# Last unit's additions of attention shared by two engines, and the next stage's weights and first block fetched during them

## What is computed

```python
xn = layernorm(x)
s = lightning_attention(xn)          # layer 0: 16 heads of 32, decayed, chunked
g = silu(bitlinear_ffn(xn))          # 512 -> 2048 -> 512, ternary weights
x = x + s * g
xn = layernorm(x)
q, k, v = xn @ wq.T, xn @ wk.T, xn @ wv.T     # layer 1: 16 heads of 32, rope on q, k
att = softmax(rope(q) @ rope(k).T / sqrt(32))
s = (att @ v) @ wo.T
gate = silu(xn @ ((wq_gate - 128) * s_gate).T)     # 512 -> 1408
up = xn @ ((wq_up - 128) * s_up).T
g = silu((gate * up) @ ((wq_down - 128) * s_down).T)
out = x + s * g
```

## Time and profile before

| what | us |
|---|---|
| runs | 3112.64, 3121.56, 3123.32 (median 3121.56) |
| the profiled execution | 3116.13 |
| its span, first to last instruction | 3114.0 |
| TensorE busy | 2878.6 (92%) |
| VectorE busy | 1842.0 (59%) |
| GpSimd busy | 1425.2 (46%) |
| ScalarE busy | 1298.4 (42%) |

### The profile page before, as it was taken

How to read it: one execution, slowest core, us unless ns; L and a number is a source line. 1 busy time by engine, 2 the same in 40 slices (tenths; PEclk the granted TensorE clock), 3 DMA queues, 4 the chain that set the end, 5 groups by cost and what they waited for, 6 DMA issues and landing times. The chain is left out here.

```text
span 3114.0 us, 54321 instructions
## 1 busy us (share of the span) xinstructions
PE 2878.6 (92%) x19392; PEld 2017.0 (65%) x19392; DVE 1842.0 (59%) x2701; ACT 1298.4 (42%) x2015; POOL 1425.2 (46%) x1006
## 2 busy tenths in 40 slices
PE   6999999699999994799999999999999669999999
PEld 5878878588888873455555555555554248788887
DVE  5657676577777653566666666666666144444444
ACT  3211111366666651255555555555555522222222
POOL 2014555122333320177777777777777812222222
PEclk9999999899999997699999999999999979999999
DMA  3211121122222323122222222222221052322221
GB/s 122 89 54 61 54 67 41 34 85 81 96 86 85 101 78 133 41 69 69 69 69 69 69 68 75 83 72 70 77 72 32 25 192 88 95 95 81 88 88 47
DMA packets 151494, 238.98 MB, mean 77 GB/s; under 512 B 13232, under 2 KB 78896, under 8 KB 151344
## 3 DMA queue, kind: packets, MB, share of 16 engines
q1 hardware_dynamic: 149904, 235.45, 22.9%
q10 hardware_dynamic: 1440, 1.33, 0.1%
HBM read 178.02 MB, written 58.72 MB: 76 GB/s over the span
## 5 line engine op out<-in xcount | busy, mean ns | idle before, releaser
L1170 DVE TENSOR_REDUCE l_attn_maxima<-l_attn_ps_max 128x2 f32<-128x1024 f32 x512 | 626.9, 1224 | 247.9 <-PE l_attn_ps_max L1222 235.6
L1143 POOL TENSOR_TENSOR l_attn_summed<-l_attn_summed,l_attn_probs 128x1024 f32<-128x1024 f32 x256 | 601.4, 2384 | 56.6 <-ACT l_attn_probs L1094 56.6
L1094 ACT ACTIVATE l_attn_probs<-l_attn_ps_sc 128x1024 f32<-128x1024 f32 x512 | 497.6, 1028 | 124.4 <-PE l_attn_ps_sc L1210 123.8
L1143 POOL TENSOR_TENSOR l_attn_summed<-l_attn_probs 128x1024 f32<-128x1024 f32 x128 | 302.8, 2391 | 334.0 <-ACT l_attn_probs L1094 334.0
L62 PE MATMUL l_attn_ps_prep<-l_attn_wqkv_hi,l_attn_xt 128*128 (+1 forms) x1024 | 286.1, 362 | 37.8 <-DMA l_attn_xt<-xt_chunks 21.3
L1423 POOL TENSOR_TENSOR l_ffn_ht_lo<-l_ffn_mixed,l_ffn_ht_hi 128x512 fp32r<-128x512 f32 x88 | 114.0, 1295 | 451.5 <-ACT l_ffn_ht_hi L1444 451.5
L1222 PEld LDWEIGHTS l_attn_ps_max<-l_attn_qk_hi 32*128 32x128 f32 x1024 | 97.2, 185 | 305.3 <-DVE l_attn_maxima L1170 294.1
L1222 PE MATMUL l_attn_ps_max<-l_attn_qk_hi 32*128 32x512 f32 x1024 | 240.0, 463 | 48.5 <-DVE l_attn_maxima L1170 25.4
L1232 PE MATMUL l_attn_ps_y<-l_attn_probs,l_attn_v 128*32 128x512 f32 x2048 | 273.4, 606 | 1.1 <-ACT l_attn_probs L1094 1.1
L1101 ACT ACTIVATE l_attn_x_tok<-l_attn_ps_prep 128x256 f32<-128x256 f32 x128 | 49.2, 385 | 445.9 <-DVE l_attn_ps_prep L1159 445.9
L62 PEld LDWEIGHTS l_attn_ps_prep<-l_attn_wqkv_hi,l_attn_xt 128*128 128x128 f32 x1024 | 185.7, 196 | 74.4 <-issue 32.1
(11 more groups left out here) (231 smaller groups left out, 6212.1 us busy)
## 6 DMA issues: line engine op xcount, KB each, us to landing
l_attn_xt<-xt_chunks SPq DMA_DIRECT2D x128, 512.0 KB, 3.6
xt_chunks<-l_ffn_xt SPq DMA_DIRECT2D x32, 512.0 KB, 4.6
l_ffn_xt<-xt_chunks SPq DMA_DIRECT2D x32, 512.0 KB, 5.9
l_attn_xin<-in_x SPq DMA_DIRECT2D x32, 256.0 KB, 4.3
...
s<-l_attn_s_sb SPq DMA_DIRECT2D x32, 256.0 KB, 2.2
...
l_ffn_xa<-in_x SPq DMA_DIRECT2D x32, 256.0 KB, 2.7
```

Of the source, the lines that this page charges most:

```text
L1094: act.activation(probs[kt % RING][:, hs, :], ps_sc[:, hs, :], ACT.Exp, scale=ATT_SCALE).then_inc(exp_done, 1)
L1143: pool.tensor_tensor(total[:, hs, :], old[:, hs, :], probs[kt % RING][:, hs, :], ALU.add).then_inc(added, 1)
L1170: dve.tensor_reduce(maxima[b][:, j, PAIR * hp:PAIR * hp + PAIR, half:half + 1], ps_max[:, :, :], AX.X, ALU.max).then_inc(max_read, 1)
```

## The change

Four things change, all in layer 1.

1. In the last unit (m = 15) the additions of a quad are shared: GpSimd adds the first pair of heads (L1143's line, now with one turn of the loop), VectorE the second (`late_add`), one step later in its program; a semaphore `added_late` counts them, and ScalarE (the exponential four steps on), and TensorE (the sum over the partitions) wait for both.
2. In ticks 16 and 17 SyncE's queue fetches gate and up in eight pieces of 128x1408 and Wo in two of 128x1024 into two buffers `ffn_raw`, and the first four chunks of x; VectorE makes the weights of them in its steps 12 to 21 (`ffn_piece`). They lie in tiles that both stages use: `w_tile` (before it holds the attention's projection weights), `x_tiles` (the attention's four `xt`), `wo_hi` and `wo_lo` (one of its two pairs of `qk`).
3. The preparation block of the feed-forward is gone. Down is fetched in four pieces in its first block and made by VectorE after j = 6, 8, 9 and 10; the scales are fetched at the stage's start by ScalarE's queue, and ScalarE and VectorE wait for all three before their first work.
4. A chunk of x is now contiguous in its tile, and the moving operand of gate and up, `x_tiles[:, :, half, k, :]`, consists of four pieces of 128 columns.

```diff
-def layer1_attention(nc, xt_in, wqkvT, rope_cos, rope_sin, yt_out, den_out):
+def layer1_attention(nc, xt_in, wqkvT, rope_cos, rope_sin, yt_out, den_out, woT, gateT, upT, x_tiles, w_tile, wo_hi, wo_lo):
...
+        FFN_PIECES = 2 * KD + 2
...
+            n = STEPS * (t - NT) + s - 12
+            return n if 0 <= n < FFN_PIECES else None
...
+            def load_raw(n):
+                need(sp, ffn_made, n - 1)
...
             def tick(t, p):
+                late = isinstance(t, int) and t >= NT
                 load(t, 0)
                 store(t - 2, 0, y_copied, y_sb, yt_out)
...
+                if late and t == NT:
+                    load_raw(0)
+                    load_raw(1)
+                    load_ahead()
+                if late and t == NT + 1:
+                    load_raw(6)
+                    load_raw(7)
                 store(t - 2, 0, den_read, den_sb, den_out)
+                if late and t == NT + 1:
+                    load_raw(8)
+                    load_raw(9)
...
                 store(t - 2, 1, den_read, den_sb, den_out)
+                if late and t == NT:
+                    for n in range(2, 6):
+                        load_raw(n)
...
-                        for i in range(HPG // PAIR):
+                        for i in range(1 if shared(m) else HPG // PAIR):
...
+            def late_add(qb, kt):
+
+                m, hs = NT - 1, slice(PAIR, HPG)
+                total = summed[qb][kt // PER_SUM]
+                need(dve, exp_done, 2 * quad_index(m, qb, kt) + 2)
...
+                dve.tensor_tensor(total[:, hs, :], old[:, hs, :], probs[kt % RING][:, hs, :], ALU.add).then_inc(added_late, 1)
+
+            def ffn_piece(n):
+
+                dve.wait_ge(raw_ld[n % 2], 16 * (n // 2 + 1))
+                if n == 0:
+                    dve.wait_ge(proj_done, CPB * NT)
+                if n < 2 * KD:
+                    dve.tensor_scalar(ffn_matrix(n), ffn_raw[n % 2][:, :], ZERO_POINT, None, ALU.subtract).then_inc(ffn_made, 1)
...
+                        if m == NT - 1 and kt % PER_SUM:
+                            late_add(qb, kt)
+                        n = ffn_piece_at(t, s)
+                        if n is not None:
+                            ffn_piece(n)
...
-                sp.dma_start(raw_o[:, :, :], w_rows(woT)).then_inc(wo_in, 16)
-                sp.dma_start(raw_gate[:, :, :], w_rows(gateT)).then_inc(gate_in, 16)
-                sp.dma_start(raw_up[:, :, :], w_rows(upT)).then_inc(up_in, 16)
-                sp.dma_start(raw_down[:, :, :], w_rows(downT)).then_inc(down_in, 16)
-                load_xt(sp, 0)
...
+        PIECE = 3
+        PIECE_AFTER = {6: 0, 8: 1, 9: 2, 10: 3}
...
+            act.dma_start(sc_down[:, :], s_down.rearrange("(a n) -> a n", a=1).to_broadcast([P, DIM])).then_inc(scales_in, 16)
+            act.wait_ge(scales_in, 48)
...
-                        mm = pe.matmul(out_bank[:, :], w[:, k, P * j:P * j + P], xt[:, half, k, :], start=(k == half == 0), stop=(k == KD - 1 and half == 1))
+                        mm = pe.matmul(out_bank[:, :].rearrange("p (c n) -> p c n", n=P), w[:, k, P * j:P * j + P], x_tiles[:, :, half, k, :], start=(k == half == 0), stop=(k == KD - 1 and half == 1))
...
-                        need(pe, xt_ld, 16 * CB * (t + 1))
+                        need(pe, xt_ld, 16 * CB * t)
...
+                    if isinstance(t, int) and t == i == 0:
+                        pe.wait_ge(down_made, len(PIECE_AFTER))
```

More of the change, by code:

```diff
@@ L973, in layer1_attention @@
         den_done, den_read, y_copied = sem("den_done"), sem("den_read"), sem("y_copied")
+        added_late, raw_ld, ffn_made, wo_hi_made, x_ahead = sem("added_late"), [sem(f"raw_ld{i}") for i in range(2)], sem("ffn_made"), sem("wo_hi_made"), sem("x_ahead")
         block = ctx.enter_context(nc.Block())
@@ L1034, in adds_with, with shared, shared_adds, ffn_matrix @@
             return ADDS * (QB * m + qb) + PAIR * ((PER_SUM - 1) * (kt // PER_SUM) + r)
+        def shared(m):
+            return isinstance(m, int) and m == NT - 1
+        def shared_adds(qb, kt):
+            return ADDS // PAIR * qb + (PER_SUM - 1) * (kt // PER_SUM) + max(kt % PER_SUM, 1)
+        FFN_PIECES = 2 * KD + 2
+        def ffn_matrix(n):
+            return w_tile[:, HID * n:HID * (n + 1)] if n < 2 * KD else None
+        def ffn_piece_at(t, s):
+            if not isinstance(t, int) or t < NT:
+                return None
+            n = STEPS * (t - NT) + s - 12
+            return n if 0 <= n < FFN_PIECES else None
         def parity(p, back):
@@ L1086, in tick @@
                         if not isinstance(m, int) or n >= RING:
-                            if qb == 0 and kt < RING:
+                            if shared(m) and (qb or kt >= RING):
+                                qb_was, kt_was = (CPB * qb + kt - RING) // CPB, (kt - RING) % CPB
+                                need(act, added, ADDS * QB * m + shared_adds(qb_was, kt_was))
+                                need(act, added_late, shared_adds(qb_was, kt_was))
+                            elif qb == 0 and kt < RING:
                                 need(act, added, adds_with(m - 1, 1, kt + RING))
@@ L1257, in prepare @@
                 else:
-                    need(pe, added, ADDS * (QB * m + i + 1))
+                    if shared(m):
+                        need(pe, added, ADDS * QB * m + ADDS // PAIR * (i + 1))
+                        need(pe, added_late, ADDS // PAIR * (i + 1))
+                    else:
+                        need(pe, added, ADDS * (QB * m + i + 1))
                     for k in range(SUMS):
@@ new lines, in load_xt, with piece_of @@
+                sp.dma_start(fp32(x_tiles[:, i, :, :, :]).rearrange("p h k n -> p (h k n)"),
+                             xt_in[src if isinstance(t, int) else sp.snap(src)]).then_inc(xt_ld, 16)
+        PIECE = 3
+        PIECE_AFTER = {6: 0, 8: 1, 9: 2, 10: 3}
+        raw_down = two("raw_down", [P, PIECE, DIM], I32)
+        raw_ld = [sem(f"raw_ld{i}") for i in range(2)]
+        down_made, scales_in = sem("down_made"), sem("scales_in")
+        def piece_of(n):
+            return slice(PIECE * n, min(PIECE * n + PIECE, KH))
@@ L1394, in store, with load_down, prologue @@
                 sp.dma_start(out_t[c if isinstance(t, int) else sp.snap(c)], res[b][:, :]).then_inc(stored[b], 16)
+            def load_down(n):
+                need(sp, down_made, n - 1)
+                ks = piece_of(n)
+                sp.dma_start(raw_down[n % 2][:, 0:ks.stop - ks.start, :], w_rows(downT)[:, ks, :]).then_inc(raw_ld[n % 2], 16)
+            def prologue():
+                for i in range(2):
+                    sp.dma_start(yt[i][:, :, :], yt_in[i]).then_inc(yt_den_ld[i], 16)
+                    sp.dma_start(den[i][:, :, :], den_in[i]).then_inc(yt_den_ld[i], 16)
+                load_down(0)
+                load_down(1)
             def tick(t, p):
```

96 lines of the change are left out of this document (52 added, 44 removed).

## The result

In the same rounds the kernel before took 3118.3 us and the changed one **3074.2 us** (medians of four runs each; 3068.8 to 3078.5), a ratio of 0.986 [0.983, 0.988]. The forecast was 3084, range 3072 to 3093.

A forecast was written before the change was run, and what follows sets the result against it. TensorE was busy 92% of the span but idle while the feed-forward's weights were transferred and waiting on GpSimd in attention's tail. 33.3 + 0.8 = 34.1 us off 3118.4 gave 3084.3, taken as 3084; range 3072 to 3093.

The forecast's parts named there:

- term 1: Start of layer 1's feed-forward: the preparation block leaves TensorE's path, 33.8 less 0.5 for a barrier, gaining 33.3 us.
- two bounds: Limits for the preparation block's gain: 33.83 us if the barrier costs nothing, 32.2 if TensorE starts 1.7 us late.
- The cover: Attention's tail and feed-forward's start: the moved fetches, conversions and scales are hidden behind other work, cost taken as 0.
- rival of a rough entry: Feed-forward's start: scales land late (2.4 us), TensorE's first product 1.7 instead of 0.5 us after the barrier; 3088, chance 0.15.
- term 2: Tail of layer 1's attention: VectorE and GpSimd share additions but exclude each other, gaining 0.8 us; range 0 to 7.1.
- nineteen instructions of the sum: Attention's tail: six GpSimd and six VectorE additions, three conversions, two casts, two subtractions, one after another, 27.7 us.
- rival of free engines: Attention's tail: VectorE and GpSimd do not exclude each other, sharing gains 7.1 us, 3078 in all; chance 0.22.
- The seams: Gate and up's four-piece operand: no cost expected; rival over 8 ns a seam is slower, chance 0.04, between without change 0.02.
- The body: Feed-forward from its first gate product to the end: no change forecast (0), matmuls 0.2325 us apart, 73 us a block.

## Why the prediction was right or wrong

- **The preparation block** (term 1): right. 33.3 us forecast, 33.8 measured (the stretch took 35.4 to 38.2 us in the other runs that keep the block). The 0.5 us that I charged for the barrier was not there: TensorE's first product starts 0.05 us behind the queue's first issue. Of the two bounds the outer one, 33.83, was met.
- **The cover.** The ten pieces cost nothing by themselves; VectorE waited up to 0.54 us for one, and the products with v kept their step of 3.33 us, but for one of 3.85, which the rows before have too (20.48 us for six). The scales landed 7.2 us after their issue, 8.04 us behind TensorE's start, and the silu that waited for them was late by 0.1 to 0.2 us, not by 2.4. The rival of a rough entry falls. (Its 2.4 is a slip: 11.3 less 9.05 is 2.25, which moves the high end of the range by 0.15.)
- **The shared additions** (term 2): the mechanism was right, the size was off: 0.8 us forecast, 1.9 measured. The nineteen instructions of the sum do follow each other, but from 2449.22 to 2475.82, in 26.6 us instead of 27.7. The sum took each at its full length; nine of them stood behind the other engine, and each of these needed 0.12 to 0.13 us less than that once released (VectorE's addition 1.08 us instead of 1.21, GpSimd's 2.24 instead of 2.36). The rival of free engines falls: with nothing else in the tail sharing gives 6.0 us, and the work on the weights takes 4.0 of them. The Trainium skill (SBUF — State Buffer, Who interferes with whom) says that either engine stands behind the other, whichever came first. No row before showed GpSimd standing; now one does (3.43 us at 2456.40 behind VectorE's 1.21, against 2.35), and the measurement agrees with it. GpSimd stands behind conversions too, as the run in which it adds everything shows: the second of its two additions at 2473.37 begins at 2476.69, 0.60 us before VectorE's cast is through (2477.29), and takes 2.84 us instead of 2.35.
- **The seams**: right: four runs of 128 columns take the time of one run of 512 (3121.7 us beside 3122.0). The runs don't test the reason given, beyond that.
- **The body** was the miss: "the product's matmuls 0.2325 us apart as now". The step that failed is in the treatment of part 4 of the change: the prediction asked what the shape of the moving operand would cost, and put the tile's new place at nothing without a reason. Eight matmuls take 1.82 us instead of 1.86, 1408 x 5 ns = 7.0 us. Moving x in the kernel before shows it. With this term the sum would have been 3118.4 - 34.1 - 7.1 = 3077.2, against 3074.2 measured.

The range held the time only because its low end was taken from another rival, the free engines, which did not happen: the forecast itself from the lowest run is 3112.6 - 34.1 = 3078.5, above the 3074.2 measured. That was luck: a right range for a wrong reason.
